# A two-layer transformer kernel: third feed-forward weight rounded in quarters inside the second attention, constant rows loaded earlier, transposes and two table loads placed earlier

## The reference

```python
x = x + L0_attn(layernorm(x))   # 16 heads of 16, biases, ALiBi slopes, causal mask, softmax
x = x + L0_ffn(layernorm(x))    # silu(x Wg) * (x Wu) then Wd; integer weights, hidden 704
x = x + L1_attn(layernorm(x))   # 16 heads of 16, causal mask, softmax, weights transposed
x = x + L1_ffn(layernorm(x))    # the same shape of FFN, hidden 768, weights rounded to float8
```

## Time and profile before

| what | us |
|---|---|
| median of three timed runs | 481.42 |
| lowest, highest | 480.17, 482.88 |
| the profiled execution: its own time | 479.32 |
| the profiled execution: its span | 477.6 |
| TensorE busy in the span | 434.1 (91%) |
| VectorE busy | 315.3 (66%) |
| ScalarE busy | 229.4 (48%) |
| GpSimd busy | 154.3 (32%) |

### The profile page before, as it was taken

How to read it: one execution, slowest core, us unless ns; L and a number is a source line. 1 busy time by engine, 2 the same in 40 slices (tenths; PEclk the granted TensorE clock), 3 DMA queues, 4 the chain that set the end, 5 groups by cost and what they waited for, 6 DMA issues and landing times.

```text
span 477.6 us, 7151 instructions
## 1 busy us (share of the span) xinstructions
PE 434.1 (91%) x2656; PEld 212.6 (45%) x2656; DVE 315.3 (66%) x624; ACT 229.4 (48%) x360; POOL 154.3 (32%) x213
## 2 busy tenths in 40 slices
PE   1899899999998989999999796999999998897997
PEld 1357543334333247434575362533343332274476
DVE  4545889998886039312235578899989882087883
ACT  4445544565665843211001540555566676724960
POOL 4454032302021121195951058232111202211780
PEclk9989999999999999999999997899999999998999
DMA  8999610000000000202001961300000000000002
GB/s 233 166 188 222 170 46 2 1 1 3 1 3 0 3 5 1 66 2 66 0 0 29 240 194 42 93 3 1 2 1 3 2 0 2 0 2 1 1 17 73
DMA packets 23894, 22.50 MB, mean 47 GB/s; under 512 B 5194, under 2 KB 23114, under 8 KB 23850
## 3 DMA queue, kind: packets, MB, share of 16 engines
q1 hardware_dynamic: 22132, 19.02, 17.7%
q0 software_dynamic: 608, 2.50, 1.8%
q10 hardware_dynamic: 1120, 0.53, 0.4%
HBM read 8.27 MB, written 1.05 MB: 20 GB/s over the span
## 4 chain that ended last, share of the span: by engine, by line
PE 66%; DVE 20%; ACT 5%; DMA 4%; issue 3%; POOL 1%; SPq 1%; DVEq 0%; ACTq 0%
DVE mx L983 12%; PE ps L647 11%; PE ps L614 10%; PE ps L629 9%; PE ps L730 9%; PE ps L769 7%; PE ps L745 5%; PE ps L735 5%; ACT prob L881 3%; PE ps L753 3%; DMA oT<-in_L_attn_Wo 3%; PE ps L617 2%; PE ps L555 1%; DVE stats L949 1%; DVE xn L1065 1%
## 5 line engine op out<-in xcount | busy, mean ns | idle before, releaser
L983 DVE TENSOR_REDUCE mx<-ps 128x1 f32<-128x512 f32 (+3 forms) x304 | 183.8, 656 | 30.0 <-PE ps L617 23.6
L881 ACT ACTIVATE prob<-ps 128x1024 f32<-128x1024 f32 (+1 forms) x192 | 146.1, 808 | 88.8 <-PE ps L629 88.1
L614 PE MATMUL ps<-kS,qS 99*128 99x512 bf16 (+7 forms) x384 | 111.3, 336 | 5.0 <-DVE mx L983 3.9
L464 POOL TENSOR_SCALAR_AFFINE_SELECT prob<-prob 128x256 f32<-128x256 f32 x128 | 51.6, 409 | 198.1 <-ACT prob L881 196.8
L629 PE MATMUL ps<-qS,kS 101*128 101x512 bf16 (+7 forms) x384 | 92.2, 330 | 2.5 <-ACT prob L881 1.6
L647 PE MATMUL ps<-prob,v 128*32 128x512 f32 (+3 forms) x768 | 81.9, 498 | 1.5 <-POOL prob L464 1.4
L614 PEld LDWEIGHTS ps<-kS,qS 99*128 99x128 bf16 (+1 forms) x384 | 35.8, 98 | 80.0 <-DVE mx L983 61.4
L617 PE MATMUL ps<-mask_q,identb 128*128 128x128 bf16 x256 | 50.2, 225 | 0.0
L629 PEld LDWEIGHTS ps<-qS,kS 101*128 101x128 bf16 (+1 forms) x384 | 31.7, 98 | 40.7 <-ACT prob L881 19.3
L730 PE MATMUL ps<-xnT,gu0T 128*128 128x512 f32 (+1 forms) x96 | 42.2, 596 | 0.7 <-ACT xnT L808 0.7
L1004 DVE COPY oT<-ps 128x512 f32<-128x512 f32 x16 | 11.0, 685 | 37.6 <-PE ps L647 37.4
(11 more groups left out here) (118 smaller groups left out, 471.5 us busy)
## 6 DMA issues: line engine op xcount, KB each, us to landing
qS<-parts SPq DMA_DIRECT2D x24, 128.0 KB, 4.6
kS<-parts SPq DMA_DIRECT2D x24, 128.0 KB, 4.0
qS<-prob SPq DMA_DIRECT2D x12, 128.0 KB, 3.8
kS<-prob SPq DMA_DIRECT2D x12, 128.0 KB, 3.4
qS<-xn SPq DMA_DIRECT2D x12, 128.0 KB, 2.4
kS<-xn SPq DMA_DIRECT2D x12, 128.0 KB, 2.5
x<-in_L_attn_x SPq DMA_DIRECT2D x2, 512.0 KB, 5.3
out<-x SPq DMA_DIRECT2D x8, 128.0 KB, 1.7
```

What stands on the lines that cost most here:

```text
L464: nc.gpsimd.affine_select(out=square, in_=square, compare_op=ALU.is_ge, fill=0.0, base=0, pattern=[[0, 2], [1, P]], channel_multiplier=-1) ...
L614: mmi = nc.tensor.matmul(span, qS[0:K_MAX[L], c, g * G + h, qt * P:(qt + 1) * P], kS[0:K_MAX[L], g * G + h, key0:key0 + keys], start=True, ...
L881: nc.scalar.activation(prob[:, n % 3, 2 * pair:2 * pair + 2, off:CH], ps[:, 2 * (m % 2):2 * (m % 2) + 2, off:CH], ACT.Exp, scale=SCALE).th ...
L983: ins = nc.vector.tensor_reduce(mx[:, slot, qt, heads[0]:heads[-1] + 1, part], src, AX_X, ALU.max)
```

## The change

Six edits:

1. In layer 1 the third weight is no longer rounded in one piece ahead of the attention. It is loaded into `parts`, the space of jobs 0 to 3, once their spreads of layer 1 have landed; VectorE cuts out the exponent bits ahead of its copy of turn 3 (`W8_DOWN_AT`); and GpSimd rounds it in four quarters of 384 columns, one ahead of the first diagonal block of each head group of chunk 1.
2. `alibi_tail` is issued directly behind x, ahead of the feed-forward weights.
3. The second four tiles of normalised x are transposed behind job 1 (`QK_FIRST` = 2), in both layers.
4. In layer 1 two side jobs instead of five run ahead of the attention; the other six go between the entries of maxima.
5. The first turn of an attention stands 7 entries ahead of the first exponential instead of 5.
6. One-element activations `warm` stand ahead of the attention (Exp) and behind its last exponential (Silu), so that the table loads stand there. In layer 0's feed-forward part `round_w8` moves one step earlier.

```diff
-QK_FIRST = 4
-V_FIRST = 5
+QK_FIRST = 2
+V_FIRST = (5, 2)
+FIRST_TURN_AHEAD = 7
+W8_DOWN_AT = 3
...
-            needed.append((at, turned[cg] + TURN_AHEAD))
+            needed.append((at, turned[cg] + (TURN_AHEAD if cg else FIRST_TURN_AHEAD)))
...
+        w8_down = [parts[:, 2 * n:2 * n + 2].rearrange("p n r q -> p (n r q)").bitcast(F32) for n in range(2)]
...
                 sp.dma_start(x[:, 4 * h:4 * h + 4, :], xin[:, 4 * h:4 * h + 4, :]).then_inc(x_in[h], 16)
+            sp.dma_start(kS[QK_ROWS:K_EXP[0], :, :], tail[0:ALIBI_ROWS[0] + MAX_ROWS]).then_inc(tail_in, 16)
+            sp.dma_start(q_flat[QK_ROWS:K_MAX[0]], tail[ALIBI_ROWS[0] + MAX_ROWS:].rearrange("r h t -> r (h t)")).then_inc(tail_in, 16)
...
+            def round_columns(w, top, dst, cols):
+                chain(nc.gpsimd.tensor_scalar(top[:, cols], top[:, cols], 2.0 ** -6, 1.5 * 2.0 ** 20, ALU.max, ALU.mult))
+                chain(nc.gpsimd.tensor_tensor(w[:, cols], w[:, cols], top[:, cols], ALU.add))
+                chain(nc.gpsimd.tensor_tensor(w[:, cols], w[:, cols], top[:, cols], ALU.subtract))
+                chain(nc.gpsimd.tensor_scalar(top[:, cols], w[:, cols], 0.55 * 2.0 ** 120, 0.0, ALU.mult, ALU.mult))
+                return nc.gpsimd.tensor_tensor(dst[:, cols], w[:, cols], top[:, cols], ALU.add)
+            def round_down(quarter):
+                if quarter == 0:
+                    pool.wait_ge(w8_exp, 3)
+                wide = HT * C // NG
+                ins = round_columns(w8_down[0], w8_down[1], d1[:, :, :].rearrange("p k i -> p (k i)"),
+                                    slice(quarter * wide, (quarter + 1) * wide))
...
                 for s in TRI:
-                    off = step_span(s)[3]
+                    g, c, kt, off, _ = step_span(s)
+                    if L == 1 and c == NC - 1 and off == 0:
+                        round_down(g)
...
+            for n in range(4):
+                pool.wait_ge(stacked[n], 16 * len(Q_PARTS) * 2)
+            pool.dma_start(w8_down[0].rearrange("p (j i) -> p j i", j=HT), w8_src[2]).then_inc(w8_in, 16)
             cut_triangles(1)
...
+                nc.scalar.activation(warm[:], nhalf[:, 0:1], ACT.Exp)
                 for s in range(N_STEP):
...
+                nc.scalar.activation(warm[:], nhalf[:, 0:1], ACT.Silu)
                 for t in range(NT):
                     bank = bank_a(("onT", L, t))
...
                     elif entry[0] == "turn":
+                        if (L, entry[1]) == (1, W8_DOWN_AT):
+                            round_w8(2)
...
-                            dve.wait_ge(w8_round, 3)
+                            dve.wait_ge(w8_round, 2)
...
-                if L == 1:
-                    round_w8(2)
                 attention(L)
...
-                        if L == 0 and ht == 3:
+                        if L == 0 and ht == 2:
                             round_w8(c)
```

More of the change, by code:

```diff
@@ L304, in two_layer_kernel @@
         nhalf = sb("nhalf", [P, NT], F32)
+        warm = sb("warm", [P, 1], F32)
         ident = sb("ident", [P, P], F32)
@@ L387, in _ @@
             sp.dma_start(d0[:, :, :].bitcast(I32), a["L0_ffn_wq_down"].rearrange("(j p) i -> p j i", p=P)).then_inc(ffn0_in, 16)
-            sp.dma_start(kS[QK_ROWS:K_EXP[0], :, :], tail[0:ALIBI_ROWS[0] + MAX_ROWS]).then_inc(tail_in, 16)
-            sp.dma_start(q_flat[QK_ROWS:K_MAX[0]], tail[ALIBI_ROWS[0] + MAX_ROWS:].rearrange("r h t -> r (h t)")).then_inc(tail_in, 16)
             for m, n in ((2, "Wv"), (3, "Wo")):
@@ L454, in _ @@
                                     pattern=[[1, P]], channel_multiplier=-1).then_inc(consts, 1)
+            def round_columns(w, top, dst, cols):
[10 more added lines that the diff above has]
+                                    slice(quarter * wide, (quarter + 1) * wide))
+                if quarter == NG - 1:
+                    ins.then_inc(w8_round, 1)
             def cut_triangles(L):
                 for s in TRI:
-                    off = step_span(s)[3]
+                    g, c, kt, off, _ = step_span(s)
+                    if L == 1 and c == NC - 1 and off == 0:
+                        round_down(g)
                     n = L * N_STEP + s
@@ L508, in _ @@
                       a["L1_ffn_down_w"].rearrange("(k p) i -> p k i", p=P)]
-            for n in range(3):
-                if n == 2:
-                    rstd_of(4)
-                    rstd_of(5)
+            for n in range(2):
                 if n:
@@ L516, in _ @@
                 pool.wait_ge(w8_exp, n + 1)
-                chain(nc.gpsimd.tensor_scalar(w8m, w8m, 2.0 ** -6, 1.5 * 2.0 ** 20, ALU.max, ALU.mult))
-                chain(nc.gpsimd.tensor_tensor(w8, w8, w8m, ALU.add))
-                chain(nc.gpsimd.tensor_tensor(w8, w8, w8m, ALU.subtract))
-                chain(nc.gpsimd.tensor_scalar(w8m, w8, 0.55 * 2.0 ** 120, 0.0, ALU.mult, ALU.mult))
-                if n < 2:
-                    dst = gu1[:, n].rearrange("p j i -> p (j i)")
-                    nc.gpsimd.tensor_tensor(dst, w8, w8m, ALU.add).then_inc(w8_round, 1)
-                else:
-                    dst = d1[:, :, :].rearrange("p k i -> p (k i)")
-                    nc.gpsimd.tensor_tensor(dst, w8, w8m, ALU.add).then_inc(w8_round, 1)
+                dst = gu1[:, n].rearrange("p j i -> p (j i)")
+                round_columns(w8, w8m, dst, slice(0, CJ * HID1)).then_inc(w8_round, 1)
+            rstd_of(4)
+            rstd_of(5)
+            for n in range(4):
+                pool.wait_ge(stacked[n], 16 * len(Q_PARTS) * 2)
+            pool.dma_start(w8_down[0].rearrange("p (j i) -> p j i", j=HT), w8_src[2]).then_inc(w8_in, 16)
             cut_triangles(1)
@@ L653, in attention @@
                 pe.wait_ge(b_free, B_AT["on", L, 0])
-                side = V_FIRST
+                side = V_FIRST[L]
                 ready = set()
@@ L779, in _ @@
                     mmi.then_inc(b_full, 1)
-                for side in range(V_FIRST):
+                for side in range(V_FIRST[L]):
                     side_job(L, side)
@@ L966, in round_w8 @@
                     dve.wait_ge(w8_round, n)
-                nc.vector.tensor_scalar(w8m.bitcast(I32), w8.bitcast(I32), 0x7F800000, None, ALU.bitwise_and).then_inc(w8_exp, 1)
+                w, top = (w8, w8m) if n < 2 else w8_down
+                nc.vector.tensor_scalar(top.bitcast(I32), w.bitcast(I32), 0x7F800000, None, ALU.bitwise_and).then_inc(w8_exp, 1)
             def add_to_x(job, L, t):
```

## The result

The changed kernel took 470.56 us in the median of four runs (469.74 to 470.80), the kernel before 482.15 us on the same chip (480.17 to 483.47): a ratio of 0.976 [0.973, 0.979]. The forecast was 471.0 us. When the same kernel ran again on another occasion, six runs gave 475.03 us (470.37 to 476.48), ratio 0.986 [0.982, 0.991]. Both lie in the range of the forecast, 466.8 to 477.

A forecast was written before the change was run, and what follows sets the result against it. VectorE's reductions of maxima and TensorE's matmuls were taken as the bound. Terms 7.75 - 0.95 + 2.2 + 0.35 = 9.35 us took the profiled 479.32 to 470.0; 1.0 added for timed runs gave 471.0, range 466.8 to 477.

The forecast's parts named there:

- the cut at turn 3: Layer 1's attention: cutting exponent bits at turn 3, where VectorE is 97% busy, loses 0.95 us.
- Layer 1, projections and first maxima: Layer 1's start: earlier second transposes and fewer v jobs ahead of the first maxima gain 3.0 us.
- the negation: Layer 1 before turn 0: without GpSimd's long two-input operation beside it, VectorE's stalled negation gains 3.2 us.
- Table load and clock: Layer 1, turn 0 to turn 1: early table load and full clock give 7.61 instead of 9.16, gain 1.55 us.
- Quarters: Layer 1, chunk 1: GpSimd's quarters of 4.3 us and a bit are covered by waits; taken as 0, at most 2.6 lost.
- The rival of a hold in chunk 1: Layer 1: quarters meet negations and the cut meets diagonals, 2.6 us back, timed 473.6; chance 0.09.
- Five or seven entries: Each attention's start: two more entries before the first turn, 0.6 gained to 1.1 us lost per layer; taken as 0.
- Layer 0: Layer 0's start: ALiBi rows issued early save part of SP's hold, gain 2.2 us, between -1.5 and 4.3.
- The rival of the rows that hold the start: Layer 0's start: early ALiBi rows hold x or Wk, first projection 9.8 us later, timed 483.0; chance 0.04.
- Feed-forward part: Layer 1's feed-forward start: the Silu table loaded ahead of use gains 0.35 us, at most 1.28.

The follow-up runs named there:

- nowarm: The changed kernel without the two extra activations that load ScalarE's tables ahead of use; 474.08 us, ratio 0.986.
- round_only: The kernel before with the quarters alone: third weight rounded by quarters inside layer 1's attention, exponent cut at turn 3; 477.90 us, ratio 0.995.
- turn5: The changed kernel with the first turn 5 entries ahead of the first exponential instead of 7; 473.00 us, ratio 0.985.
- after_again: The changed kernel, unchanged, run on another occasion; 475.03 us, ratio 0.986.
- tail_back: The changed kernel with the two loads of ALiBi rows put back behind the feed-forward weights; 472.16 us, ratio 0.982.
- tail_pad: The changed kernel with the ALiBi rows padded in memory, so transfers are cut into 2 KB pieces instead of 32 KB; 471.71 us, ratio 0.981.
- qk4: The changed kernel with the second transposes behind job 3, as in the kernel before; 474.63 us, ratio 0.984.
- one_piece: The changed kernel without quarters, the third weight rounded in one piece ahead of layer 1's attention; 472.42 us, ratio 0.979.
- v5: The changed kernel with five v jobs instead of two ahead of layer 1's first maxima; 474.14 us, ratio 0.981.
- tail_last: The changed kernel with all eight constant rows loaded last of the first loads, behind bo; 469.62 us, ratio 0.977.
- ones_half: The changed kernel with q's three rows of ones set by GpSimd and VectorE, k's five rows loaded behind bo; 466.59 us, ratio 0.971.

## Why the prediction was right, point by point

**Sum.** Predicted for the profiled execution 9.35 us, measured in the span 8.70 (477.58 to 468.88). That the sum came so close is in part luck, for four of its terms were off and cancel. Counted along the trace, layer 0 gave 0.42 us up to layer 1's first projection (I had 2.2), the way from there to turn 0 6.56 (6.2), from turn 0 to turn 1 0.85 (1.55), the cut at turn 3 -0.87 (-0.95), and the feed-forward part 1.78 (0.35).

**Layer 1, projections and first maxima (3.0) and the negation (3.2).** Together 6.2 predicted, 6.56 measured up to turn 0. Taken back one by one, the second transposes are worth 4.35 us (I said 2.3: the 1.7 of the clock was missing), the v jobs 0.69 (I had 3.0 - 2.3 = 0.7), the quarters 0.59; added alone to before, the quarters are worth 3.21. The parts don't add up, because with the other edits in, the long operations miss the negation. That the hold goes with the long operation was right; that it is worth 3.2 us was right only in the order of before.

**Table load and clock (1.55).** The step failed, and something else gave 0.85 in its place. The load never set this stretch (in nowarm turn 1 is where it is in after), and the clock stayed low (0.52 over 287 to 294). The spacing goes with the entries: it is 9.16 us in before, 9.16 in round_only and 9.18 in turn5, which have five, whatever the clock (0.77 and twice 0.84 over 283 to 305), and with seven 8.31, or 7.33 to 7.98 where the clock has 0.92 (after_again, tail_back, tail_pad, qk4). One kernel with seven does not fit: one_piece took 8.77 at a clock of 0.84, and there the second negation was held too, 0.79 us, by a GpSimd operation of 3.44 us.

**Quarters.** The cut costs what was said: from turn 1 to turn 7 layer 1 takes 94.71 us instead of 93.84, 0.87 against 0.95. A quarter took 5.3 us, not 4.3 and a bit, and none was waited for; chunk 1 lost nothing. The rival of a hold in chunk 1 did not occur.

**Five or seven entries (0).** The step that was most off: both bounds (0.6 gained, 1.1 lost a layer) were too narrow. In layer 1 the two entries cost nothing up to turn 0 (28.84 and 28.85 us) and are worth 0.87 behind it; in layer 0 five left TensorE waiting 3.03 us for a spread, in the one profile that there is; with seven it waited 2.27 in one_piece, so their worth there is open.

**Layer 0 (2.2).** The number came at turn 0, 1.99 us, the reason did not, and the number is luck. The five profiled executions with the early rows, the early second transposes and seven entries (after, after_again, nowarm, v5, one_piece) have turn 0 at 52.5 us on average, the two of before's layer 0 at 51.3. No gain of layer 0 from these edits is shown. I had SP's held issues as what is saved; they grew, to 9.23 us. "x is ahead in the same queue, and Wk is half through by then" was wrong: x's second half was held 3.4 us in the first profile, Wk some 10 in the second. What paid for it in the first profile was the gap of TensorE with its clock (24 projections in 10.47 us), and the transfers behind the rows, which ran at 269 instead of 187 GB/s. At layer 1's first projection only 0.42 of the gain was left, by the half clock in the output projection. That occurs in after, after_again and nowarm and in none of the other profiles; what calls it is open, and `warm` does not, as nowarm shows.

**The rival of the rows that hold the start.** I gave it 0.04 and 483.0 us. Its mechanism came true in two of seven executions, with 10.4 us at Wk where I had 9.8 (16.4 from issue to landing instead of 6.0); its price did not. The first projection was 9.2 us later than before, turn 0 only 3.3, since the transfers behind the rows then ran fast (layer 1's Wo took 5.1 us from issue to landing, in before 12.1). So such an execution takes some 475, not 483. I had charged the hold in full and taken layer 0's gain away as well.

**Feed-forward part (0.35, at most 1.28).** Mis-sized: 1.78. The load was worth 1.27, the bound that I had put at the edge: TensorE waits later for VectorE's bank (nowarm: 1.51 us where after has 0.24). The other 0.5 us is a half clock that before had there (0.92 over 421 to 442 us) and after not. The split depends on which is taken first. tail_back, tail_pad, tail_last and qk4 have `warm` and that half clock, and take 47.02 to 47.47 us, 0.13 to 0.58 less than before. So at before's clock the load was worth about the 0.35 that I gave, and what I left out is the clock.

## What to carry to other kernels

- The loads of rows into few partitions held what was beside them here, not only what was behind. Put such a load where nobody waits for a transfer, and write constant rows with an idle engine instead of loading them.
- Before GpSimd gets work, look which VectorE operations of two inputs or of fp32 TENSOR_SCALAR run beside it. Two memsets of 7 us in the wrong place cost 6.8 us at layer 0's turn 0 against after, over half of what the whole change had brought.
- A gap of TensorE is worth more than its length where the clock falls in it (2.43 us of gap, 4.35 us of time). And where a change touches the first loads, profile the same kernel more than once: a single profile can show a start of 12 us or one of 21, and the match of one stage with its forecast can be luck.

## What the runs showed of the hardware

- While eight constant rows are in flight early, the core's DMA moves 64 to 95 GB/s at a share of 0.97 to 1.15 (the windows 8 to 12 and 12 to 16 us of eight profiles); in the same windows of the six without them 283 to 351 GB/s at 1.06 to 1.38.
- Pieces of 2 KB instead of 32 KB leave that rate about as it is (87 and 95 GB/s in tail_pad).
- GpSimd's memset holds VectorE's fp32 TENSOR_SCALAR for its whole length (0.4 us became 7.1); VectorE's statistics beside a GpSimd memset (0.39 to 0.43 us in ones_half) and its reductions of maxima beside GpSimd's five operations (before) keep their pace.
- The same kernel has some of its half-clock stretches in different places from one execution to the next (after and after_again behind turn 0 of layer 1: 8.31 and 7.33 us to turn 1). One that falls on busy TensorE cost 1.0 to 1.7 us here. Totals of single profiles that differ by less than that say nothing of an edit.
